# One-hot operands read from PSUM, and products evicted in halves, in the adjacency build of a GNN kernel

## The reference, cut to what matters

```python
edge_index = jnp.stack([src, dst])
x = _layernorm(x + L0(x, ..., src, dst, edge_type_3, node_type_3))   # typed messages, segment_sum over dst
x = _layernorm(x + L1(x, ..., edge_index, edge_weight))              # segment_sum of edge_weight * support[col]
x = _layernorm(x + L2(edge_index, x))                                # normalised sum over the edges
x = _layernorm(x + L3(x, edge_attr_64, src, dst, ...))               # (edge_feat @ W + h[src]), segment_sum over dst
```

## Time and profile before

| | us |
|---|---|
| median of 3 runs | 5168.8 (5166.46 to 5170.2) |
| the profiled execution's own time | 5166.42 |
| its span | 5164.6 |
| PE, DVE, POOL, ACT busy in the span | 3645.9, 3255.0, 2201.7, 1201.7 |
| first and last gather of line 1394 | 635.2, 2387.2 |
| first and last one-hot product of DVE, line 1421 | 633.7, 2100.8 |
| first instruction of the next block on ACT | 2403.7 |

### The profile page before, as it was taken

How to read it: one execution, slowest core, us unless ns; L and a number is a source line. 1 busy time by engine, 2 the same in 40 slices (tenths; PEclk the granted TensorE clock), 3 DMA queues, 4 the chain that set the end, 5 groups by cost and what they waited for, 6 DMA issues and landing times. The chain is left out here.

```text
span 5164.6 us, 99803 instructions
## 1 busy us (share of the span) xinstructions
PE 3645.9 (71%) x38930; PEld 2640.2 (51%) x38930; DVE 3255.0 (63%) x4527; ACT 1201.7 (23%) x2110; POOL 2201.7 (43%) x2050
## 2 busy tenths in 40 slices
PE   4457755555555555102888887399999599989997
PEld 3345655555555555102777776255555244444444
DVE  7886899999999999202777775766666500230022
ACT  0015655555555555100000000300000200010000
POOL 0051277777777777775777775000000003000300
PEclk9998899999999999656999999699999799989998
DMA  9646799999999999758878777288886367656664
GB/s 315 222 106 226 259 316 334 349 347 344 354 342 345 352 348 345 266 157 156 230 228 229 228 230 181 92 320 305 301 308 250 121 202 228 200 164 201 218 190 138
DMA packets 710790, 1297.10 MB, mean 251 GB/s; under 512 B 367384, under 2 KB 512428, under 8 KB 701260
## 3 DMA queue, kind: packets, MB, share of 16 engines
q1 hardware_dynamic: 579516, 823.86, 49.2%
q10 hardware_dynamic: 60300, 314.88, 15.5%
q0 software_dynamic: 70576, 152.66, 11.7%
HBM read 814.90 MB, written 529.03 MB: 260 GB/s over the span
## 5 line engine op out<-in xcount | busy, mean ns | idle before, releaser
L1394 POOL DMA_INDIRECT big<-typed_msgs,big x1216 | 1374.6, 1130 | 402.4 <-issue 365.7
L1439 PE MATMUL psum<-big 128*128 128x98 bf16 x7936 | 844.9, 206 | 607.3 <-DVE big L1421 567.7
L1439 PEld LDWEIGHTS psum<-big 128*128 128x128 bf16 x7936 | 761.3, 96 | 659.7 <-DVE big L1421 615.1
L2081 PE MATMUL psum<-big 128*128 128x512 bf16 (+1 forms) x4704 | 992.4, 374 | 82.5 <-DMA big<-adj 82.5
L1440 PE MATMUL psum<-big 128*128 128x49 bf16 x7936 | 831.4, 189 | 0.1
L1441 PE MATMUL psum<-big 128*128 128x49 bf16 x7936 | 829.0, 185 | 1.6 <-issue 1.6
L1441 PEld LDWEIGHTS psum<-big 128*128 128x128 bf16 x7936 | 782.0, 99 | 2.2 <-issue 2.1
L2081 PEld LDWEIGHTS psum<-big 128*128 128x128 bf16 x4704 | 460.4, 98 | 606.0 <-DMA big<-adj 83.0
L1440 PEld LDWEIGHTS psum<-big 128*128 128x128 bf16 x7936 | 765.6, 96 | 0.8 <-issue 0.7
L1666 PE MATMUL psum<-big 128*128 128x192 f32 x3648 | 643.8, 331 | 124.1 <-DMA big<-typed_msgs,big 105.1
L1891 PE MATMUL psum<-big 128*128 128x416 f32 x1984 | 656.4, 494 | 63.5 <-DVE big L1925 62.4
(11 more groups left out here) (318 smaller groups left out, 2799.0 us busy)
## 6 DMA issues: line engine op xcount, KB each, us to landing
wadj<-big ACTq DMA_DIRECT2D x248, 784.0 KB
big<-wadj SPq DMA_DIRECT2D x124, 1568.0 KB, 7.0
big<-adj SPq DMA_DIRECT2D x210, 896.0 KB, 4.8
big<-staged SPq DMA_DIRECT2D x304, 384.0 KB, 4.1
staged<-big SPq DMA_DIRECT2D x60, 1920.0 KB
adj<-big ACTq DMA_DIRECT2D x62, 1568.0 KB
big<-edge_feats SPq DMA_DIRECT2D x456, 128.0 KB, 4.2
edge_feats<-in_edge_attr SPq DMA_DIRECT2D x1, 51562.5 KB, 161.6
```

What stands on the lines that cost most here:

```text
L1394: pool.indirect_dma_start(out=sgot4[:, c, u, 0:D], out_offset=None, in_=typed_rows, in_offset=bass.IndirectOffsetOnAxis(ap=pairs4i[:, g, u ...
L1439: pe.matmul(to[:, 0:2 * NB], lo, hi_b[:, q, t, 0:2, 0:NB], start=True, stop=False)
L2081: last = pe.matmul(ps[c % 2][:, 0:len(blocks) * P], terms_[:, k, b * D:(b + 1) * D], ring_a[:, m % RA, 0:len(blocks), s * P:(s + 1) * P], ...
```

## The change

The three one-hot instructions of DVE read one of their two operands from PSUM. Behind the clearing of PSUM, DVE copies both ramps, as 89 words, to the last words of banks 6 and 7, and ACT, once it has made `terms` in SBUF, copies these 384 words to the start of bank 6 or 7 (a new third copy in `double`). Two banks are thereby lost to the products: these go to three regions of two banks, each with eight nodes, at 98 columns a node in place of 128. PE and ACT work by half a batch. `s_mm_b` and `s_adj_e` count halves, so the numbers waited for are doubled, that of POOL's gate too. ACT's part of the loop is written out, since the number of the region is no longer the same in each pass.

```diff
         def made_in(q):
-            return psum[:, q * 2048:(q + 1) * 2048].rearrange("p (t c) -> p t c", c=P)
+            return psum[:, q * 1024:(q + 1) * 1024].rearrange("p (k x) -> p k x", k=2)[:, :, 0:4 * 2 * NB].rearrange("p k (t c) -> p k t c", c=2 * NB)
+        REGIONS, HALF = 3, TT // 2
+        RAMP_WORDS, TERM_WORDS = (P + HC) // 2, 3 * SLOTS
+        def ramp_words(k):
+            return psum[:, (7 + k) * 512 - RAMP_WORDS:(7 + k) * 512]
+        def term_words(k):
+            return psum[:, (6 + k) * 512:(6 + k) * 512 + TERM_WORDS]
...
-                            at_least(pool, s_mm_b, i * (2 * BATCHES) + c * (2 * BATCHES) // SPER - BEHIND)
+                            at_least(pool, s_mm_b, 2 * (i * (2 * BATCHES) + c * (2 * BATCHES) // SPER - BEHIND))
...
                 dve.wait_ge(s_clear, 3)
+                for k in range(2):
+                    dve.tensor_copy(ramp_words(k), both_ramps).then_inc(s_clear, 1)
+                dve.wait_ge(s_clear, 5)
...
-                            parts = terms[:, k, b * TT:(b + 1) * TT, :, :]
+                            parts = term_words(k).bitcast(BF16).rearrange("p (g r d) -> p g r d", r=3, d=2)[:, b * TT:(b + 1) * TT, :, :]
-                            at_least(dve, s_mm_b, n - 1)
+                            at_least(dve, s_mm_b, n * 2 - 2)
-                            dve.tensor_tensor(hi, in_twos(hi_ramp).to_broadcast([P, TT, HC // 2, 2]), all_columns(sbk, HC),
+                            dve.tensor_tensor(hi, in_twos(psum_ramps(k)[1]).to_broadcast([P, TT, HC // 2, 2]), all_columns(sbk, HC),
-                                              in_twos(lo_ramp).to_broadcast([P, TT, P // 2, 2]), all_columns(sl, P), ALU.is_equal)
+                                              in_twos(psum_ramps(k)[0]).to_broadcast([P, TT, P // 2, 2]), all_columns(sl, P), ALU.is_equal)
...
+                def half_batch(n, half):
+                    q, m = n % 2, 2 * n + half
+                    if half == 0:
                         pe.wait_ge(s_hot_b, n + 1)
-                        at_least(pe, s_adj_e, n - 1)
+                    at_least(pe, s_adj_e, m + 1 - REGIONS)
+                    for j in range(HALF):
+                        t = half * HALF + j
+                        to = made_in(m % REGIONS)[:, j // 4, j % 4, :]
...
+                    act.wait_ge(s_twice, i * 4 + (2 * k + 1))
+                    act.copy(term_words(k), terms[:, k, :, :, :].rearrange("p g r d -> p (g r d)").bitcast(F32)).then_inc(s_twice, 1)
...
+                act.wait_ge(s_clear, 5)
                 double(0, 0, None)
...
-                            act.wait_ge(s_mm_b, i * (2 * BATCHES) + (k * BATCHES + b + 1))
-                            act.copy(adj_st[:, k, :, b * TT:(b + 1) * TT],
-                                     made_in(b % 2)[:, :, 0:NB].rearrange("p t s -> p s t"))
+                            for half in range(2):
+                                m = 2 * (i * (2 * BATCHES) + k * BATCHES + b) + half
+                                act.wait_ge(s_mm_b, m + 1)
+                                made = made_in(m % REGIONS)
+                                t0 = b * TT + half * HALF
+                                act.copy(adj_st[:, k, :, t0:t0 + HALF].rearrange("p s (c t) -> p s c t", c=2),
+                                         made[:, :, :, 0:NB].rearrange("p c t s -> p s c t"))
...
-                block_pairs(act, body)
+                for i in range(GB // 2):
+                    body(i)
```

More of the change, by code:

```diff
@@ L1239, in build @@
         hi_b = c.bitcast(BF16).rearrange("p (k t s c) -> p k t s c", k=2, s=4, c=HC)
-        c, at = cut(at, (P + HC + 1) // 2)
-        c = c.bitcast(BF16)
+        both_ramps, at = cut(at, (P + HC) // 2)
+        c = both_ramps.bitcast(BF16)
         lo_ramp, hi_ramp = c[:, 0:P], c[:, P:P + HC]
@@ L1348, in made_in, with psum_ramps @@
         def made_in(q):
-            return psum[:, q * 2048:(q + 1) * 2048].rearrange("p (t c) -> p t c", c=P)
+            return psum[:, q * 1024:(q + 1) * 1024].rearrange("p (k x) -> p k x", k=2)[:, :, 0:4 * 2 * NB].rearrange("p k (t c) -> p k t c", c=2 * NB)
+        REGIONS, HALF = 3, TT // 2
+        RAMP_WORDS, TERM_WORDS = (P + HC) // 2, 3 * SLOTS
+        assert HC % 2 == 0 and RAMP_WORDS + TERM_WORDS <= 512
+        def ramp_words(k):
+            return psum[:, (7 + k) * 512 - RAMP_WORDS:(7 + k) * 512]
+        def psum_ramps(k):
+            both = ramp_words(k).bitcast(BF16)
+            return both[:, 0:P], both[:, P:P + HC]
+        def term_words(k):
+            return psum[:, (6 + k) * 512:(6 + k) * 512 + TERM_WORDS]
         with nc.Block() as block:
@@ L1428, in _ @@
             def _(pe):
[L1429 to L1433, removed]
+                pe.wait_ge(s_clear, 5)
+                def half_batch(n, half):
+                    q, m = n % 2, 2 * n + half
+                    if half == 0:
                         pe.wait_ge(s_hot_b, n + 1)
-                        at_least(pe, s_adj_e, n - 1)
[L1436 to L1444, removed]
+                    at_least(pe, s_adj_e, m + 1 - REGIONS)
+                    for j in range(HALF):
+                        t = half * HALF + j
+                        to = made_in(m % REGIONS)[:, j // 4, j % 4, :]
+                        lo = lo_b[:, q, t, :]
+                        pe.matmul(to[:, 0:2 * NB], lo, hi_b[:, q, t, 0:2, 0:NB], start=True, stop=False)
+                        pe.matmul(to[:, NB:2 * NB], lo, hi_b[:, q, t, 2, 0:NB], start=False, stop=False)
+                        last = pe.matmul(to[:, NB:2 * NB], lo, hi_b[:, q, t, 3, 0:NB], start=False, stop=True)
+                    last.then_inc(s_mm_b, 1)
+                for n in range(NBATCH):
+                    for half in range(2):
+                        half_batch(n, half)
             @block.scalar
@@ L1477, in body @@
                         for b in range(BATCHES):
-                            act.wait_ge(s_mm_b, i * (2 * BATCHES) + (k * BATCHES + b + 1))
-                            act.copy(adj_st[:, k, :, b * TT:(b + 1) * TT],
-                                     made_in(b % 2)[:, :, 0:NB].rearrange("p t s -> p s t"))
-                            act.copy(wadj_st[:, k, b // 2, :, b % 2 * TT:(b % 2 + 1) * TT],
-                                     made_in(b % 2)[:, :, NB:2 * NB].rearrange("p t s -> p s t")).then_inc(s_adj_e, 1)
+                            for half in range(2):
+                                m = 2 * (i * (2 * BATCHES) + k * BATCHES + b) + half
[4 more added lines that the diff above has]
+                                         made[:, :, :, 0:NB].rearrange("p c t s -> p s c t"))
+                                act.copy(wadj_st[:, k, b // 2, :, t0 % 32:t0 % 32 + HALF].rearrange("p s (c t) -> p s c t", c=2),
+                                         made[:, :, :, NB:2 * NB].rearrange("p c t s -> p s c t")).then_inc(s_adj_e, 1)
                             if k == 1:
@@ L1645, in _ @@
             def _(pe):
-                pe.wait_ge(s_clear, 5)
+                pe.wait_ge(s_clear, 7)
                 def turn(i, own_):
```

8 lines of the change are left out of this document (4 added, 4 removed).

## The result

| | before | after |
|---|---|---|
| median | 5169.5 us (5166.46 to 5171.41, 4 runs) | 5076.8 us (5075.28 to 5080.47, 4 runs) |
| profiled execution, its span | 5166.42, 5164.6 | 5076.37, 5074.6 |
| last one-hot product of DVE | 2100.8 | 2276.65 |
| last gather of the block | 2387.2 | 2274.5 |
| first instruction of the next block | 2403.7 | 2314.0 |

The ratio is 0.9826, with a 95% interval of 0.9814 to 0.9838: faster by 1.7%. The next block starts 89.8 us earlier and the profiled execution is 90.05 us shorter, so all of it comes from the build.

What follows compares the result with a forecast made beforehand. DVE and DMA engines fill the build, but POOL's staging ends the block; once released, 1634 us of DMA work at 1.02 ends it 164 us earlier, less 3 for the start: 5166.4 - 161 = 5005, said as 5006, range 4930 to 5095.

Steps and rivals of the forecast that it cites:

- the main case: Whole block: DMA engines late next at a share of 1.02, 5006 us; own range 4959 to 5053; chance 0.56.
- the rival of starving gathers: Build keeps its pace, engines serve ACT's large stores first; next block at 2311, 93 us earlier, 5074; chance 0.12.
- DVE's operands release POOL: One SBUF input per one-hot instruction: free gather pitch of 1.245 us, POOL's end at 2153, 235 us earlier.
- DVE's own time: Three one-hot instructions keep 567, 1215 and 1398 ns with a PSUM operand: nothing added; other end 2.44 us a batch.
- The first rival: DVE's one-hot instructions fall to one element a cycle: 2.44 us a batch more, 6090 us; chance 0.13.
- ACT: Evictions by halves: 1.8 us a batch in place of 1.6, below 2.96, hidden; costed at nothing.
- Start: ACT doubles the first tables only after PSUM is cleared: about 3 us later for the build.
- The regions: PE's three half regions absorb 3.0 us of a wait in place of 3.7; up to 25 us at 35 waits.
- The work is fixed: DMA queues from 635 to 2401 us: 1634 us of work of the 16 engines, unchanged as the block shortens.
- The share of 1.02: DMA share over the block: 1634/1.02 = 1602 us, end at 2237 in place of 2401, 164 us earlier.
- The sign of DVE's idle time: DVE idle in the build for some 100 us, before the first instruction of a batch, ended by PE.
- A share at or above 1.0 to the end: Sign of being right: DMA share at or above 1.0 to the block's end, no long tail of POOL alone.

Runs made afterwards that it cites:

- SP's order: Padding-rows kernel, with SP loading features for a ring half behind its next store, not ahead: 4996.7 us against 5170.1 for the kernel before, ratio 0.9667.
- The padding rows: Changed kernel with padding slots of the edge list gathering different rows in place of row 0: 5026.8 us against 5170.1 for the kernel before, ratio 0.9722.
- ACT's stores earlier: Changed kernel with padding rows, SP's order and ACT's last two stores a batch earlier: 5094.8 us against 5164.7 for the kernel before, ratio 0.986.

## Why the prediction was right, and where it was off

It said 5006, with 4930 to 5095; measured were 5076.8. The mechanism was right and one term of the sum was off, by more than the main case allowed for. The main case's own range ended at 5053, and the measured time lies in the wider one only because that took in the rival of starving gathers (5074), whose price it nearly has and whose mechanism did not occur: the build ended at 2278 and not at 2101. That part of the hit is luck.

- **DVE's operands release POOL: right.** Gathers at 0.94 to 0.95 with 0.30 between them from the first on; shown as the cause by the run with the operands back in SBUF (0.9994).
- **DVE's own time: right.** 569, 1213 and 1393 ns, within 0.4% of the earlier trace rows. The first rival's price was nil. The Trainium skill's table (VectorE: DVE Perf Modes, The perf-mode tier table: tensor_tensor with any PSUM operand at 1x) does not hold for these bf16 operands; its other page (Vector Engine (DVE) Microarchitecture Reference, 5.1 Performance modes) fits.
- **ACT: right.** A batch's four instructions take 1.74 us (1199.10 to 1200.84 in the changed kernel), against 1.8.
- **Start: right.** From the block before to PE's first matmul it takes 12.45 us (623.00 to 635.45) and took 10.06 (625.22 to 635.28): 2.4 us, against 3.
- **The regions: the cover was about as large as said, the waits were not.** Of ACT's 393.9 us of waits 185.8 reach DVE, so 3.5 us are absorbed each time, against 3.0. But there are 59 waits in place of 35, of 6.7 us on the mean.
- **The work is fixed: right.** 1637 us against 1634.
- **The share of 1.02: wrong, and this is the 70 us.** The block ran at 0.977: about 0.99 to 2190 us and 0.89 behind it. 1637/0.977 is 1675 us in place of 1602, 73 us more, where the measured time is 71 above the forecast. From 635 to 2190 us the work done is 1637 - 0.89 x 120 = 1530; at 1.02 that is 1500 us and not 1555, so 55 us lie there and some 15 in the end.

The prediction argued 1.02 as a value between a mean of 0.99 and a 10 us window of 1.06, with ACT's dry queue in mind. The windows after show why the mean can't come near the peak: 1.05 while ACT's stores are queued, and 0.74 on the mean for the 5 us about each release of ACT, when its queue is empty and SP stands behind a store with its loads. The runs name the two parts. SP's order gives 0.99 to 1.02 in the body. The padding rows give the end: there q0 took 37.9% of the engines for 2.17 MB, and POOL stood still for 13 and 28 us. With both mended the kernel takes 4996.7 us, and in its profiled execution the block ends at 2232.8, where the prediction had put 2237. That doesn't bear out its share for the changed kernel: this version has some 25 us less work, and over its whole block the share is 1.01. The prediction had no term of its own for the way from the jobs' end to the next block. That way took 36 us at a share of 0.79 (2278 to 2314 us) and not 15.6, since ACT's stores now come last; it is part of the 15 us.

The sign of DVE's idle time was right and its size was not (190.5 us, expected about 100), which is the same term. "A share at or above 1.0 to the end" was the sign that failed, and with it "the next block at about 2240". Of the rivals, starving is real, but only with ACT's stores earlier. What no part of the forecast had is that the kernel before itself can take 13 to 14% longer, with PE the one that is waited for: there the ratio is 1.0064.

## What to carry to other kernels

When an engine is held by another's SBUF reads, moving one operand of every such instruction to PSUM releases it; here one instruction of three left out kept most of the lock. When the released work lands on full DMA engines, forecast with the mean share that the stretch has had, not with the best window, and look at what the last transfers are: their rate need not be that of the others. Two jobs that share the DMA engines are best when they end together, and an order that helps one can cost more than it gives.

## What the runs showed of the hardware that was not expected

- Bf16 tensor_tensor with one operand in PSUM runs at the rate of SBUF operands: 1393 ns for 2400 elements against 1398, 569 for 800 against 567. The f32 rows with a PSUM input cost twice that per element.
- A gather that starts inside a DVE instruction with both inputs in SBUF ends 0.82 us after it; one that starts beside an operand in PSUM takes 0.94, and so does one that was running when such an instruction began.
- Gathers of one same DRAM row cost 14 us of the 16 engines per MB, those of different rows 3.1.
- The same program takes 5165 to 5170 us in some sittings and 5841 to 5915 in others. In the latter PE waits for nothing that the profile shows in 313.7 us of 1300, at a granted clock of 0.63 in place of 0.90. Whether it is the chip, and what it is, was not found.
